# Attention layers of a graph network: other softmax groups, and four pieces of work moved in their engines' orders

## The chip, the cores and the metric

The kernel runs on one core of one Trainium2 chip. A core has five engines that run side by side, each through its own list of instructions, in order: TensorE (PE in the profile, its weight loads PEld), VectorE (DVE), ScalarE (ACT), GpSimd (POOL) and SyncE (SP). They wait for each other on semaphores. The metric is the time of one execution in device microseconds (us). Before the change it is 5247.03 us, the median of 3 runs (5243.42 to 5260.6).

## The reference, cut to what matters

A network of four graph layers over 50000 nodes of 128 features and 25000 edges. The first one is five attention layers (GAT), and only their code is changed. Each of the five computes, with a self loop at every node:

```python
def _gat_layer(x, src, dst, edge_attr_full, W, att, b, ew, eb):
    edge_emb = edge_attr_full @ ew.T + eb
    xw = x @ W
    xj = xw[src].reshape(-1, H, D) + edge_emb.reshape(-1, H, D)
    xi = xw[dst].reshape(-1, H, D)
    alpha = einsum(xi, att_i) + einsum(xj, att_j)     # two heads
    alpha = leaky_relu(alpha, 0.2)
    amax = segment_max(alpha, dst)
    ea = exp(alpha - amax[dst])
    denom = segment_sum(ea, dst)
    alpha = ea / (denom[dst] + EPS)
    aggr = segment_sum(xj * alpha[..., None], dst)
    return aggr.mean(axis=1) + b
for l in range(5):
    h = _gat_layer(h, ...)
    if l < 4: h = relu(h)
```

The edges are sorted by destination. So the softmax over a node's edges is a running maximum and a running sum along the list, and a node's row is needed only where it has edges.

## The kernel before, in words

The 25000 edges lie in 196 tiles of 128, and two tiles make a pair: a layer works through 98 pairs. The layers run one after the other, each in a block of its own (`gat_layer`, called five times), because a layer gathers the rows that the last one has written.

Pair by pair, "step i" of each engine:

- GpSimd gathers the source row of each edge, one indirect DMA for a tile, two for a pair, into a ring of 24 pairs (`RG`). It waits only for a free place in the ring, and each group of pairs has its own semaphore (`g_in`).
- SyncE loads the nodes' own rows (`load_own`), five pairs ahead, stores result rows, and for each group loads masks and edge features (`load_group`), in layers 2 to 5 also the values at run ends (`load_fill_of`), and stores statistics (`store_ends`).
- ScalarE in step i evicts the aggregation of pair i (`evict`), applies ReLU to the mix of pair i-1 (`relu`), evicts edge sums, copies the rows of pair i-2 (`to_rows`), for one step of a group takes exp, and then multiplies gathered rows by their softmax weights (`weigh`), up to two pairs in a step and at most four pairs ahead.
- VectorE makes one-hot matrices of the edges' places (`one_hot`, eight pairs ahead), adds the node's own part (`with_own`), and copies pieces.
- TensorE in step i multiplies weighted rows by one-hots (`aggregate`, L1716), sums edge features in bursts (`sum_edges`), mixes pair i-1 with the weights (`mix`, L1744 and L1745) and turns pair i-2 to rows (`to_rows`, L1757).

The softmax is not made pair by pair but for a group of pairs, one lane for each tile and head, so that up to 56 lanes of VectorE share one instruction. `GAT_PAIRS` lists the groups' sizes. Group g+1 is made ready while group g is worked on, at steps that `GAT_STEPS` sets, counted within group g: at "source" VectorE adds the scores of the gathered rows (`source_scores`, L1358, for which all gathers of group g+1 must have landed) and TensorE turns them (`turn_scores`, L1700); at "scores" VectorE computes the running maximum (`scores`, L1395 to L1401) and ScalarE exp (L1588); at "weights" VectorE computes sums and quotients (`weights`, L1408 to L1417) and TensorE turns them (`turn_weights`, L1706); at "take" VectorE copies them out of PSUM (`take_weights`, L1424). Only then can ScalarE weigh (L1599). Group 0 is prepared before the loop, with nothing beside it. In TensorE's step the turning of the weights stands behind `aggregate` and ahead of `mix`. ScalarE weighs pairs of the next group from the step ahead of "weights". The own scores of a group (`own_scores`) are made in the second step of the group before.

There is no planner: each engine's loop is written out in Python, and the tables above and the places of the calls set the order.

Of the kernel before, what the change touches and what calls it, by code (L numbers as in the profile page):

```python
# [15 lines left out]
P = 128  # L16
# [1140 lines left out]
EdgeBurst = namedtuple("EdgeBurst", "first pairs group")  # L1157
GAT_PAIRS = (4, 12, 14, 14, 14, 14, 14, 12)
GAT_STEPS = ((1, 2, 3, 3), (8, 9, 11, 11), (9, 10, 12, 13), (8, 9, 11, 12), (6, 8, 10, 11), (5, 7, 9, 10), (5, 7, 9, 10), (0, 0, 0, 0))

# [8 lines left out]
def edge_bursts(C):  # L1169

    most = GM // 2
    out = []
    for g, G in enumerate(softmax_groups(C)):
        for k in range(0, G.pairs, most):
            out.append(EdgeBurst(G.first + k, min(most, G.pairs - k), g))
    return out


def gat_layer(nc, K, I, l):
# [3 lines left out]
    NP = C // 2  # L1183
    groups, bursts = softmax_groups(C), edge_bursts(C)
# [9 lines left out]
    with ExitStack() as ctx:  # L1194
# [55 lines left out]
        with nc.Block(no_gpsimd_drain=True) as block:  # L1250
# [86 lines left out]
            def _(eng):  # L1337
                step = Order(eng, s.step)
                eng.memset(aggE[:, :, 2 * P:4 * P], 0.0).then_inc(s.padded, 1)
                eng.memset(prE[:, :, :, :, :], 0.0).then_inc(s.zeroed, 1)  # L1340
                if l > 0:
# [4 lines left out]
                    back = seq4[:, ::-1]  # L1346
                    eng.tensor_tensor_scan(back, K.q.goes[0:4, ::-1], back, 0.0, ALU.mult, ALU.add).then_inc(s.seq, 1)

                def source_scores(g):
# [147 lines left out]
                def runs_weights():  # L1497
# [6 lines left out]
                    eng.tensor_tensor(AS, EL, AS, ALU.mult).then_inc(s.weights, 1)  # L1504

                own_scores(0)
                own_scores(1)
                for i in range(EARLY):
                    one_hot(i)
                source_scores(0)  # L1510
# [72 lines left out]
            def _(eng):  # L1583
# [68 lines left out]
                for i in range(NP + 2):  # L1652
# [16 lines left out]
                    if i < NP:  # L1669
                        if steps_at(g, k, "scores"):  # L1670
                            exp(g + 1)
                        for _ in range(2):
                            if weighed_to < NP and weighed_to <= i + 4 and (at(weighed_to)[0] == g or k >= groups[g].steps["weights"] - 1):
                                weigh(weighed_to)
                                weighed_to += 1
# [11 lines left out]
            def _(eng):  # L1687
# [76 lines left out]
                for i in range(NP + 2):  # L1764
                    if i < NP:
# [7 lines left out]
                        if steps_at(g, k, "source"):  # L1773
                            turn_scores(g + 1)
                        if steps_at(g, k, "weights"):
                            turn_weights(g + 1)
                    if i == NP - 6:
# [19 lines left out]
                    if 2 <= i:  # L1797
                        to_rows(i - 2)

                eng.wait_ge(s.px, NP)  # L1800
# [1631 lines left out]
```

## Time and profile before

| | us |
|---|---|
| median of 3 runs | 5247.03 |
| the profiled execution, its own time | 5250.73 |
| its span | 5249.0 |
| TensorE busy | 4269.4 |
| VectorE busy | 4034.0 |
| ScalarE busy | 3328.7 |
| GpSimd busy | 3228.0 |
| the five attention layers, from 1571 to 3401 us | 1830 |

A layer takes 363 to 369 us. In the third (2302 to 2671) TensorE is busy 303.8 us, VectorE 260.7, ScalarE 255.8, GpSimd 213.1, and the granted TensorE clock is 0.93 of full. The page counts instructions by line of the kernel; "L806" is the helper of all gathers. A row of the timeline gives the start from the beginning of the span, the length, the engine, the line, what is written and read, and in brackets how long the engine had been idle and what ended that.

### The profile page before, as it was taken

Reading aid. Unit: us, or ns where it says so; the run is one execution under the profiler, and the core shown is the slowest. Engines: PE = TensorE matmul, PEld = TensorE weight load, DVE = VectorE, ACT = ScalarE, POOL = GpSimd, SP = SyncE. Lnnn points to the kernel's source line nnn. Section 1 sums busy time; section 2 is a strip of 40 time slices with the busy share of each in tenths; the row PEclk is TensorE's granted clock in tenths of the full one; section 3 lists DMA queues with packets and bytes.
Section 4 is the critical chain, followed back from the end, with each engine's and each line's share of the span. In section 5 each row is a group of like instructions: output and inputs, shape, how many; then the busy total and the mean of one; then the engine's idle time right before and its main releaser. Section 6 shows DMA issues by size and latency. Waiting matters only on the chain. (4 is left out here: it accounts for less than half of the span.)

```text
span 5249.0 us, 101811 instructions
## 1 busy us (share of the span) xinstructions
PE 4269.4 (81%) x28013; PEld 3696.3 (70%) x28013; DVE 4034.0 (77%) x14947; ACT 3328.7 (63%) x9065; POOL 3228.0 (61%) x2905
## 2 busy tenths in 40 slices
PE   4899999999976978969969959877895868879575
PEld 4777777778866867858858848644775857757475
DVE  5799999999986767767757767687566968859765
ACT  2777777777755857847847848644774547768400
POOL 2888888877777727637457367222752247666277
PEclk6999999999988989989989979955997989989755
DMA  3999997666645646636636546488773759857332
GB/s 91 186 221 221 221 220 221 220 221 207 212 155 127 144 86 132 135 77 142 128 89 141 113 102 148 100 246 239 163 144 85 198 158 246 242 125 134 72 94 85
DMA packets 1107279, 825.55 MB, mean 157 GB/s; under 512 B 209510, under 2 KB 1068202, under 8 KB 1106396
## 3 DMA queue, kind: packets, MB, share of 16 engines
q1 hardware_dynamic: 1026800, 690.47, 50.7%
q0 software_dynamic: 77040, 128.08, 12.7%
q8 instruction: 235, 3.85, 0.3%
q14 instruction: 324, 2.65, 0.2%
q10 hardware_dynamic: 2880, 0.50, 0.1%
HBM read 374.78 MB, written 448.11 MB: 157 GB/s over the span
## 5 line engine op out<-in xcount | busy, mean ns | idle before, releaser
L806 POOL DMA_INDIRECT gat_G<-table,k_src_row x980 | 1072.8, 1095 | 316.5 <-issue 282.2
L1599 ACT ACTIVATE gat_Gw<-gat_G,gat_al 128x128 f32<-128x128 f32 x1960 | 618.5, 394 | 88.9 <-DVE gat_al L1424 88.9
L1455 DVE SCALAR_TENSOR_TENSOR gat_Gw<-gat_own,gat_al,gat_Gw 128x128 f32<-128x128 f32 x1960 | 554.7, 343 | 69.2 <-ACT gat_Gw L1599 69.0
L1716 PE MATMUL gat_psG<-gat_ends_at,gat_Gw 128*128 128x128 f32 x3920 | 538.1, 282 | 43.7 <-DVE gat_Gw L1455 43.6
L1744 PE MATMUL gat_psZ<-gat_aggT,t_gat_wh 128*128 128x256 f32 x1960 | 526.3, 392 | 15.3 <-ACT gat_hT L1625 14.9
L1716 PEld LDWEIGHTS gat_psG<-gat_ends_at,gat_Gw 128*128 128x128 f32 x3920 | 493.4, 197 | 54.9 <-DVE gat_Gw L1455 51.9
L635 PEld LDWEIGHTS nodes_psR<-t_ident_v,nodes_hTl 128*128 128x128 f32 x3168 | 431.7, 192 | 105.5 <-issue 1.8
L635 PE MATMUL nodes_psR<-t_ident_v,nodes_hTl 128*128 128x132 f32 x3168 | 446.1, 278 | 0.0
L479 POOL TENSOR_TENSOR nodes_rstd<-nodes_var,k_half 128x14 f32<-128x14 f32 x140 | 365.7, 2612 | 127.0 <-DVE nodes_var L546 127.0
L1625 ACT ACTIVATE gat_hT<-gat_psZ,t_gat_bias 128x256 f32<-128x256 f32 x490 | 231.1, 472 | 267.4 <-PE gat_psZ L1745 261.9
L1744 PEld LDWEIGHTS gat_psZ<-gat_aggT,t_gat_wh 128*128 128x128 f32 x1960 | 340.1, 194 | 56.1 <-ACT gat_aggT L1606 17.2
L1606 ACT ACTIVATE gat_aggT<-gat_psG 128x512 f32<-128x512 f32 x490 | 285.8, 583 | 41.0 <-PE gat_psG L1716 30.8
L1745 PE MATMUL gat_psZ<-gat_aggE,t_gat_ewT 128*128 128x256 f32 x980 | 299.1, 388 | 0.0
L806 POOL DMA_INDIRECT nodes_xg<-in_x,first_dst_tm x196 | 194.8, 994 | 144.6 <-POOLq L84 95.8
L730 ACT ACTIVATE nodes_rows<-nodes_psR 128x396 f32<-128x396 f32 x528 | 263.3, 499 | 30.4 <-PE nodes_psR L635 5.2
L719 ACT ACTIVATE nodes_hTl<-nodes_psY,t_gat_bias 128x384 f32<-128x384 f32 x264 | 153.2, 580 | 178.5 <-PE nodes_psY L645 157.7
L484 POOL DMA_INDIRECT row_of<-first_slot_row_tm,k_node_tm x196 | 222.9, 1137 | 59.7 <-issue 59.4
L1757 PEld LDWEIGHTS gat_psR<-t_ident_v,gat_hT 128*128 128x128 f32 x1568 | 240.5, 193 | 20.5
L523 DVE TENSOR_SCALAR nodes_n<-nodes_xs,nodes_negmean,nodes_rstd 128x128 f32<-128x128 f32 x792 | 245.3, 399 | 4.5 <-issue 2.3
L806 POOL DMA_INDIRECT hgt_edge_G<-table,k_src_row x196 | 186.7, 953 | 100.6 <-ACT hgt_edge_hm L2144 53.5
L806 POOL DMA_INDIRECT cat_edge_G<-table,k_src_row x196 | 194.0, 990 | 84.6 <-ACT cat_edge_hm L2144 41.4
L3189 POOL DMA_INDIRECT out<-cat_sums_rows,k_node_tm x196 | 198.5, 1013 | 77.4 <-issue 57.3
(672 smaller groups left out, 12721.8 us busy)
## 6 DMA issues: line engine op xcount, KB each, us to landing
table<-nodes_rows SPq DMA_DIRECT2D x660, 198.0 KB
table<-nodes_n SPq DMA_DIRECT2D x396, 192.0 KB
gat_own<-table SPq DMA_DIRECT2D x490, 132.0 KB
table<-gat_rows SPq DMA_DIRECT2D x392, 132.0 KB
nodes_x<-in_x SPq DMA_DIRECT2D x132, 192.0 KB
out<-nodes_x_out SPq DMA_DIRECT2D x132, 192.0 KB
gat_G<-table,k_src_row POOLq DMA_INDIRECT x980
hgt_q<-enter_q SPq DMA_DIRECT2D x98, 144.0 KB, 2.2
```

Of the source, the lines that this page charges most:

```text
L479: eng.tensor_tensor(rstd[:, k % 4, :], var[:, k % 4, :], K.half[:, 0:M], ALU.pow).then_inc(s.pow, 1)
L523: ins = eng.tensor_scalar(to[:, t, 0:D], of[:, t, :], negmean[:, k % 4, at + t:at + t + 1], rstd[:, k % 4, at + t:at + t + 1], ALU.add, AL ...
L635: mm = eng.matmul(psR[n % 2][:, t * ROWW:(t + 1) * ROWW], hTl[l][:, t * P:(t + 1) * P], K.ident_v[:, l, :], start=True, stop=True)
L730: eng.activation(rows[:, l - 1, b % 2, :, :], wide(psR[n % 2], T, ROWW), ACT.Copy).then_inc(s.rows_out, 1)
L806: eng.indirect_dma_start(to, None, table, bass.IndirectOffsetOnAxis(ap=index, axis=0)).then_inc(sem, 16)
L1455: ins = eng.scalar_tensor_tensor(Gw[:, i % RS, t, h, :], own[:, i % RO, t, 0:D], al[:, g % 2, 1, a:a + 1], Gw[:, i % RS, t, h, :], ALU.mul ...
L1599: ins = eng.activation(Gw[:, i % RS, t, h, :], G[:, i % RG, t, 0:D], ACT.Copy, scale=al[:, g % 2, 0, a:a + 1])
L1606: eng.activation(aggT[:, i % RA, :, :, :].rearrange("p t h q -> p (t h q)"), psG[i % 2][:, :], ACT.Copy).then_inc(s.aggT, 1)
L1716: mm = eng.matmul(o[:, h * P:(h + 1) * P], Gw[:, i % RS, t, h, :], ends_at[:, i % RE, t, :], start=True, stop=True)
L1744: eng.matmul(o, K.gat_wh[:, l, h, :], aggT[:, i % RA, :, h, :], start=(h == 0), stop=False)
L1745: eng.matmul(o, K.gat_ewT[:, l, k % EDGE_ROWS, :], aggE[:, b % 2, c:c + 2 * P], start=False, stop=True).then_inc(s.mixed, 1)
L1757: mm = eng.matmul(o, of, K.ident_v[:, l + 1, :], start=True, stop=True)
```

## The change

It does five things, all in the attention layers:

- Groups: 4, 6, 9, 11, 12 and four of 14 pairs in place of 4, 12, five of 14 and 12: nine groups for eight, with new steps for them. For groups of 4 and of 14 pairs the step tables are partly those of before.
- Bursts of edge sums are cut into equal parts (`edge_bursts`), so 9 pairs make 4 and 5, not 7 and 2.
- VectorE: the eight early one-hots come ahead of the own scores of groups 0 and 1, and the two memsets behind the sequence scan.
- TensorE: the weights are turned at the end of the step, behind `mix` and `to_rows`.
- ScalarE: pairs of the next group are weighed from the step "take" on, not from the step ahead of "weights".

```diff
-GAT_PAIRS = (4, 12, 14, 14, 14, 14, 14, 12)
-GAT_STEPS = ((1, 2, 3, 3), (8, 9, 11, 11), (9, 10, 12, 13), (8, 9, 11, 12), (6, 8, 10, 11), (5, 7, 9, 10), (5, 7, 9, 10), (0, 0, 0, 0))
+GAT_PAIRS = (4, 6, 9, 11, 12, 14, 14, 14, 14)
+GAT_STEPS = ((1, 2, 3, 3), (3, 4, 5, 5), (5, 6, 7, 8), (7, 8, 9, 10), (7, 8, 10, 11), (8, 9, 11, 12), (6, 8, 10, 11), (5, 7, 9, 10), (0, 0, 0, 0))
...
     for g, G in enumerate(softmax_groups(C)):
-        for k in range(0, G.pairs, most):
-            out.append(EdgeBurst(G.first + k, min(most, G.pairs - k), g))
+        n = (G.pairs + most - 1) // most
+        for k in range(n):
+            a, b = G.pairs * k // n, G.pairs * (k + 1) // n
+            out.append(EdgeBurst(G.first + a, b - a, g))
...
                 step = Order(eng, s.step)
-                eng.memset(aggE[:, :, 2 * P:4 * P], 0.0).then_inc(s.padded, 1)
-                eng.memset(prE[:, :, :, :, :], 0.0).then_inc(s.zeroed, 1)
                 if l > 0:
                     eng.memset(seq4[:, :], 0.0).then_inc(s.seq, 1)
...
                     eng.tensor_tensor_scan(back, K.q.goes[0:4, ::-1], back, 0.0, ALU.mult, ALU.add).then_inc(s.seq, 1)
+                eng.memset(aggE[:, :, 2 * P:4 * P], 0.0).then_inc(s.padded, 1)
+                eng.memset(prE[:, :, :, :, :], 0.0).then_inc(s.zeroed, 1)
...
+                for i in range(EARLY):
+                    one_hot(i)
                 own_scores(0)
                 own_scores(1)
-                for i in range(EARLY):
-                    one_hot(i)
                 source_scores(0)
...
-                            if weighed_to < NP and weighed_to <= i + 4 and (at(weighed_to)[0] == g or k >= groups[g].steps["weights"] - 1):
+                            if weighed_to < NP and weighed_to <= i + 4 and (at(weighed_to)[0] == g or k >= groups[g].steps["take"]):
                                 weigh(weighed_to)
...
                             turn_scores(g + 1)
-                        if steps_at(g, k, "weights"):
-                            turn_weights(g + 1)
...
                     if 2 <= i:
                         to_rows(i - 2)
+                    if i < NP and steps_at(g, k, "weights"):
+                        turn_weights(g + 1)
```

TensorE, first layer, the last step of group 0 and the start of group 1. L1716 (L1718 after) aggregates a pair, L1706 (L1708) turns the weights, L1744, L1745 and L1757 (two lines later after) mix and make rows, L1731 sums edge features, L1695 turns own scores. Before:

```order
L1716 MATMUL gat0_psG1<-gat0_ends_at,gat0_Gw 128x128 x4
L1706 MATMUL gat0_psT<-k_ident,gat0_alB 128x48 x2
L1744 MATMUL gat0_psZ<-gat0_aggT,t_gat_wh 128x256 x2
L1745 MATMUL gat0_psZ<-gat0_aggE,t_gat_ewT 128x256
L1757 MATMUL gat0_psR1<-t_ident_v,gat0_hT 128x132 x2
L1716 MATMUL gat0_psG0<-gat0_ends_at,gat0_Gw 128x128 x4
L1731 MATMUL gat0_psE1<-gat0_ends_at,gat0_wex 32x128 x14
L1695 MATMUL gat0_psT<-k_ident,t_sc_a 56x128 x2
```

After:

```order
L1718 MATMUL gat0_psG1<-gat0_ends_at,gat0_Gw 128x128 x4
L1746 MATMUL gat0_psZ<-gat0_aggT,t_gat_wh 128x256 x2
L1747 MATMUL gat0_psZ<-gat0_aggE,t_gat_ewT 128x256
L1759 MATMUL gat0_psR1<-t_ident_v,gat0_hT 128x132 x2
L1708 MATMUL gat0_psT<-k_ident,gat0_alB 128x24 x2
L1718 MATMUL gat0_psG0<-gat0_ends_at,gat0_Gw 128x128 x4
L1733 MATMUL gat0_psE1<-gat0_ends_at,gat0_wex 32x128 x12
L1697 MATMUL gat0_psT<-k_ident,t_sc_a 36x128 x2
```

The turning of the weights has moved behind the mix and the rows, and holds 24 lanes instead of 48.

VectorE at the start of the second layer. L1376 to L1387 (two lines later after) are own scores, L1441 (L1443) the one-hots, L1358 the scores of gathered rows. Before:

```order
L1376 TENSOR_TENSOR gat1_vb<-gat1_psT,gat1_mk 48x256
L1379 SCALAR_TENSOR_TENSOR gat1_vb<-gat1_mk,gat1_vb 48x128 x2
L1383 SCALAR_TENSOR_TENSOR gat1_vb<-gat1_mk,gat1_fill,gat1_vb 48x128 x4
L1386 SCALAR_TENSOR_TENSOR gat1_lp<-gat1_vb,t_lane_c 48x128
L1387 SCALAR_TENSOR_TENSOR gat1_lp<-gat1_lp 48x128
L1441 TENSOR_TENSOR gat1_ends_at<-k_iota,k_endpos 128x256 x8
L1358 TENSOR_TENSOR gat1_sq<-gat1_G,t_edge_sc 128x16
```

After:

```order
L1348 MEMSET gat1_aggE 128x2x256
L1349 MEMSET gat1_prE 128x256
L1443 TENSOR_TENSOR gat1_ends_at<-k_iota,k_endpos 128x256 x8
L1378 TENSOR_TENSOR gat1_vb<-gat1_psT,gat1_mk 16x256
L1381 SCALAR_TENSOR_TENSOR gat1_vb<-gat1_mk,gat1_vb 16x128 x2
L1385 SCALAR_TENSOR_TENSOR gat1_vb<-gat1_mk,gat1_fill,gat1_vb 16x128 x4
L1388 SCALAR_TENSOR_TENSOR gat1_lp<-gat1_vb,t_lane_c 16x128
L1389 SCALAR_TENSOR_TENSOR gat1_lp<-gat1_lp 16x128
```

The one-hots have moved from behind the own scores of both groups to ahead of them, with the memsets just ahead.

ScalarE, first layer, from exp of group 3 to the weighing of its first pairs (L1599, L1601 after; x4 is one pair, x8 two). L1606 evicts an aggregation, L1625 is ReLU, L1634 the row copy. Before, in group 2 of 14 pairs:

```order
L1588 ACTIVATE gat_ee<-gat_ee 56x256
L1606 ACTIVATE gat_aggT<-gat_psG 128x512
L1625 ACTIVATE gat_hT<-gat_psZ,t_gat_bias 128x256
L1634 ACTIVATE gat_rows<-gat_psR 128x264
L1599 ACTIVATE gat_Gw<-gat_G,gat_al 128x128 x8
L1606 ACTIVATE gat_aggT<-gat_psG 128x512
```

After, in group 2 of 9 pairs:

```order
L1590 ACTIVATE gat_ee<-gat_ee 44x256
L1608 ACTIVATE gat_aggT<-gat_psG 128x512
L1627 ACTIVATE gat_hT<-gat_psZ,t_gat_bias 128x256
L1636 ACTIVATE gat_rows<-gat_psR 128x264
L1608 ACTIVATE gat_aggT<-gat_psG 128x512
L1627 ACTIVATE gat_hT<-gat_psZ,t_gat_bias 128x256
L1636 ACTIVATE gat_rows<-gat_psR 128x264
L1601 ACTIVATE gat_Gw<-gat_G,gat_al 128x128 x8
L1608 ACTIVATE gat_aggT<-gat_psG 128x512
```

One more step of evictions now stands between exp and the weighing.

## Rows read from the trace of the kernel before

**Rows 1.** Waits of the layers, 1571 to 3400: total, times, longest.

```profile
DVE gat_sq L1358 <- DMA gat_G<-table,k_src_row: 153.2, 24, 19.1
...
PE gat_psT L1706 <- DVE gat_alB L1417: 79.6, 40, 6.1
```

**Rows 2.** Timeline, third layer, a regular step: start, length, engine, line.

```profile
2388.78 0.41 DVE L1441 TENSOR_TENSOR gat_ends_at<-k_iota,k_endpos 128x256 f32<-128x256 f32 x1
...
2389.12 1.12 DVE L1455 SCALAR_TENSOR_TENSOR gat_Gw<-gat_own,gat_al,gat_Gw 128x128 f32<-128x128 f32 x4
...
2390.49 1.05 PE L1716 MATMUL gat_psG<-gat_ends_at,gat_Gw 128*128 128x128 f32 x8
...
2391.39 1.03 PE L1744 MATMUL gat_psZ<-gat_aggT,t_gat_wh 128*128 128x256 f32 x4
...
2393.13 1.05 PE L1716 MATMUL gat_psG<-gat_ends_at,gat_Gw 128*128 128x128 f32 x8
...
2393.33 0.39 ACT L1634 ACTIVATE gat_rows<-gat_psR 128x264 f32<-128x264 f32 x1
```

**Rows 3.** Timeline: scores of gathered rows, groups 0 and 1 of layer 1, group 1 of layer 3.

```profile
1583.45 0.18 DVE L1358 TENSOR_TENSOR gat_sq<-gat_G,t_edge_sc 128x16 f32<-128x16 f32 x1 [1.49 <-DMA gat_G<-table,k_src_row]
...
1613.76 0.21 DVE L1358 TENSOR_TENSOR gat_sq<-gat_G,t_edge_sc 128x48 f32<-128x48 f32 x1 [19.11 <-DMA gat_G<-table,k_src_row]
...
2345.80 0.21 DVE L1358 TENSOR_TENSOR gat_sq<-gat_G,t_edge_sc 128x48 f32<-128x48 f32 x1 [15.36 <-DMA gat_G<-table,k_src_row]
```

**Rows 4.** Timeline, third layer, the edges behind groups 1 and 2.

```profile
2390.98 0.40 ACT L1588 ACTIVATE gat_ee<-gat_ee 56x256 f32<-56x256 f32 x1
...
2392.70 0.41 DVE L1408 TENSOR_TENSOR_SCAN gat_f<-gat_mk,gat_ee 56x128 f32<-56x128 f32 x1
...
2395.41 0.32 DVE L1417 TENSOR_TENSOR gat_alB<-gat_alB,gat_mk 56x128 f32<-56x128 f32 x1
...
2396.46 2.45 ACT L1599 ACTIVATE gat_Gw<-gat_G,gat_al 128x128 f32<-128x128 f32 x8 [2.74 <-DVE gat_al L1424]
...
2399.00 1.16 PE L1716 MATMUL gat_psG<-gat_ends_at,gat_Gw 128*128 128x128 f32 x8 [0.94 <-DVE gat_Gw L1455]
...
2406.80 1.16 PE L1716 MATMUL gat_psG<-gat_ends_at,gat_Gw 128*128 128x128 f32 x8 [0.88 <-DVE gat_Gw L1455]
...
2439.05 2.45 ACT L1599 ACTIVATE gat_Gw<-gat_G,gat_al 128x128 f32<-128x128 f32 x8 [3.82 <-DVE gat_al L1424]
...
2442.48 1.72 PE L1744 MATMUL gat_psZ<-gat_aggT,t_gat_wh 128*128 128x256 f32 x4 [1.97 <-ACT gat_hT L1625]
```

**Rows 5.** Timeline, third layer: aggregation of pairs 4, 58 and 97.

```profile
2359.49 1.82 PE L1716 MATMUL gat_psG<-gat_ends_at,gat_Gw 128*128 128x128 f32 x8
...
2532.18 1.05 PE L1716 MATMUL gat_psG<-gat_ends_at,gat_Gw 128*128 128x128 f32 x8
...
2648.17 1.05 PE L1716 MATMUL gat_psG<-gat_ends_at,gat_Gw 128*128 128x128 f32 x8
```

**Rows 6.** Timeline: last gather and last scores of layers 1, 3 and 5.

```profile
1844.87 0.94 POOL L806 DMA_INDIRECT gat_G<-table,k_src_row  x1 [0.30 <-issue]
...
1849.45 0.28 DVE L1358 TENSOR_TENSOR gat_sq<-gat_G,t_edge_sc 128x40 f32<-128x40 f32 x2 [1.01 <-DMA gat_G<-table,k_src_row]
...
2573.95 0.94 POOL L806 DMA_INDIRECT gat_G<-table,k_src_row  x1 [0.30 <-issue]
...
2587.27 0.28 DVE L1358 TENSOR_TENSOR gat_sq<-gat_G,t_edge_sc 128x40 f32<-128x40 f32 x2
...
3314.85 1.01 POOL L806 DMA_INDIRECT gat_G<-table,k_src_row  x1 [0.30 <-issue]
...
3320.93 0.27 DVE L1358 TENSOR_TENSOR gat_sq<-gat_G,t_edge_sc 128x40 f32<-128x40 f32 x2
```

**Rows 7.** Timeline, third layer: one gather and VectorE beside it.

```profile
2568.62 1.08 DVE L1434 TENSOR_TENSOR gat_wex<-gat_ex,gat_al 128x896 f32<-128x896 f32 x1
2568.62 2.23 POOL L806 DMA_INDIRECT gat_G<-table,k_src_row  x1 [0.30 <-issue]
```

## The prediction

> **What bounds the kernel now.** I read the page first and then only the five attention layers, since the change touches nothing else. The profiled execution took 5250.7 us (span 5249.0); the three timed runs had a median of 5247.0, so I work in the profiled execution and take 3.7 off at the end. "k" is the place of a pair in its group, "weights of g" the softmax of group g.
>
> I then looked for what TensorE and VectorE wait for in the layers. VectorE waits 153.2 us for gathered rows, in 24 waits, and TensorE 79.6 us for softmax weights in 40 waits [rows 1]. Next I took the third layer in order of time. TensorE repeats a step of 2.64 us for each pair (starts 2390.49 and 2393.13) with no gap in it: here TensorE is the bound [rows 2]. Two things break the rhythm. One is the start: after two pairs VectorE sits 15.36 us until the 32 gathers of groups 0 and 1 have landed, in the first layer 19.11 us [rows 3]. The other is the edge between groups: there the softmax chain runs through VectorE, ScalarE, VectorE, TensorE, VectorE, ScalarE and VectorE before TensorE has work again [rows 4]. From the first pair of group 1 (pair 4, 2359.49) to pair 58 (2532.18) 172.7 us pass for 54 pairs [rows 5]; 54 x 2.64 is 142.6, so the edges cost 30.1 us there.
>
> There is a second bound beside TensorE: the stream of 196 gathers of each layer. It runs ahead nearly free, and the last group's scores cannot be made before it has landed. In the first layer this is the limit already (last gather issued at 1844.87, VectorE goes on at 1849.45 after 1.01 us of waiting); in the third the scores come at 2587.27, 13.3 us after the last issue at 2573.95, and did not wait [rows 6].
>
> **The change, part by part (third layer).**
>
> *Smaller first groups.* Group 1 needs 20 gathers landed in place of 32. 24 gathers took 1613.76 - 1583.45 = 30.3 us in the first layer, 1.26 each [rows 3], so 12 fewer are 15.2 us: VectorE's scores of group 1 come at 2330.6 instead of 2345.80. Then the old chain took 13.7 us to the first pair of group 1 (2359.49). In the new order TensorE turns the weights after a mix and a row product (from 2391.39 to the next aggregation at 2393.13, 1.7 us, [rows 2]), which then stand between; most of it lies in its wait for the weights, and I charge 0.6. Pair 4 starts at 2330.6 + 14.3 = 2344.9, which is 14.6 us earlier.
>
> *What a group costs TensorE beyond 2.64 us a pair.* Its first two pairs take 2406.80 - 2399.00 = 7.8 us instead of 5.3 [rows 4]: 2.5, with the first burst of edge sums, the turning of own scores and 0.9 of waiting for VectorE's own scores. A second burst (1.1) and the turning of scores (0.3) make 3.9, or 2.8 for the six-pair group with one burst.
> The end of a group is where the table of steps decides. ScalarE's exp stands behind the row copy, 3.2 us after TensorE's start of that pair (2393.33 + 0.39 against 2390.49, [rows 2]), exp 0.4 more, and the weights on VectorE 3.0 (2392.70 to 2395.73; exp and these in [rows 4]). With the weights one step after the scores, as in new groups 1, 2 and 3, VectorE has to wait for exp: the pair after takes place 3.65 + 3.0 + 1.6 (one-hot 0.4, own part 1.1, [rows 2]) = 8.3 us after the scores' pair instead of 5.3, so 3.0. With the take in the last step, as in new groups 1 to 4, ScalarE can weigh the next group's first pair only behind its row copy of the last pair: 3.2, then from there weighing, own part and aggregation as between 2396.46 and 2399.00, 2.6; 5.8 us instead of 2.64, so 3.2. I get for groups 1 to 5: 8.4 (both in one step, and VectorE enters without a lead: 5.6 + 2.8), 10.2, 10.2, 8.6, 5.1: 42.5 us over their 52 pairs.
> So pair 56 starts at 2344.9 + 52 x 2.64 + 42.5 = 2524.7. Before, pair 58 started at 2532.18, so pair 56 at about 2526.9. Of the 14.6 us gained at the start some 2 are left: before, groups 1 to 4 paid 30.1 us, now five groups pay 42.5.
>
> *Weights turned at the end of the step.* The 79.6 us in 40 waits hold five starts; of the rest TensorE fills up to 1.7 us each with a mix and a row product. Where the next pair hangs on the weights (take last) this gives nothing, since those products lay in the bubble before too. After pair 56 it gives about 0.7 at each of two edges. Cover gone: were the weights ready earlier, their turning would come up to 1.7 us late, and VectorE's take with it.
>
> *Weighing from the step of taking.* Before, ScalarE stood 3.82 us at the weighing with its evictions behind it, and TensorE then waited 1.97 for ReLU output [rows 4]. That wait goes. In groups that take in the last step the weighing itself is the path (the 3.2 above), and I have counted that. For the later groups (take in step 10 of 14) nothing changes, because the window of four pairs ahead opens there anyway.
>
> *One-hots first, memsets later.* Eight one-hots (0.4 us each, [rows 2]) and two memsets move into VectorE's wait for masks; group 0 starts about 3 us sooner in layers 2 to 5. But scores of group 1 then wait for gathers until 2330.6 anyway, so I take nothing; it is 0 to 1 us.
>
> *One more group.* One more set of mask, edge and statistic transfers on SyncE's queue, which own rows and result rows share, and one more set of VectorE's softmax work; where the path sees them they are in the group costs, and SyncE loads own rows five pairs ahead. Lanes fall from 48 to 24 in group 1, which scans do not reward.
>
> From pair 58 to pair 97 the old kernel took 2648.17 - 2532.18 = 116.0 us [rows 5]; the new one has 41 pairs from pair 56: 116.0 + 5.3 - 1.4 = 119.9, so pair 97 starts at 2644.6, 3.6 us earlier.
>
> *Clock.* In [rows 4] the mix at 2442.48 has 1.72 us for the four products that take 1.03 in [rows 2]: TensorE was granted 1.2 GHz there instead of 2.4 after its waits at the edge. The new kernel has two more edges with such waits; at 0.7 for the mix and, as an estimate from it, 0.5 for the products behind it I charge one of them, 1.2 us. The Trainium skill, "TensorE: Matmul & The Clock Gate", section "HAM oscillation", says that a kernel which idles between bursts falls to half clock again and again; by it every new edge would pay, 1.2 us more a layer than I charge. The trace agrees for some edges (here) and not for others: [rows 4] has one at full clock at 2399.00.
>
> The layer comes to -3.6 + 1.2 = -2.4 us. I take it for layers 2, 3 and 4: -7.2. Layer 1 ends on its gathers before and after: -0.5. Layer 5 has only a little room before its gathers (scores at 3320.93, last gather issued at 3314.85, [rows 6]): -2. Sum -9.7; 5250.7 - 9.7 = 5241.0, less 3.7 for the median: **5237 us**.
>
> **Rivals.** A gain or loss within 0.3% (15.7 us, about what a measurement of this kernel can tell from none) is no change.
> *Gathers are the bound and the edges cost little.* For it: VectorE and TensorE overlap more than my chains allow, and the first groups' steps stand close to when their gathers land. Then each layer ends on the last gather: landing 4.6 us after issue (1844.87 to 1849.45), the scores can come at 2578.5 instead of 2587.27 in layer 3 (8.7) and at 3319.4 instead of 3320.93 in layer 5 (1.5); half-way between, 5.1, in layers 2 and 4, none in layer 1: 20.3 us, **5227**. With landings 2 us shorter and layers 2 and 4 like layer 3 it would reach 5214.
> *The gather stream gets longer.* Row: a gather beside the weighted edge features (VectorE, 1.08 us) took 2.23 us, against 0.94 for the one at 2573.95 [rows 6, 7]. VectorE's work now begins to press the stream some 15 us sooner, while its amount up to the last gather stays: at most 2 us a layer, which cancels the forecast: **5247**. The skill's page "SBUF — State Buffer", section "Who interferes with whom", would have it otherwise: it says that tensor_tensor does not stall the descriptors of such a DMA; by it this rival is void. The row speaks against the page.
> *Slower.* Place: the edges of new groups 1 to 4. If each of these four falls to 1.2 GHz after its wait (where I charged one more), three more at 1.2 us and VectorE, without a lead, passing on 1 us at each, that is +6.6 a layer against -2.4: +4 in four layers, and in layer 1 its end stays; 5247 + 17 = **5264**. It decides from the point where the edges of groups 1 to 5 cost over 46 us together. Against it: the third layer now has edges at full clock.
> *The change does not do what it says*: the first stall only moves to the scores of group 2 or 3. Against it: the 40 further gathers of groups 2 and 3 end at 2330.6 + 40 x 1.26 = 2381, and TensorE comes to the step of those scores (pair 15) at 2344.9 + 11 x 2.64 + 8.4 + 3.6 = 2386. This is close; its price is under 2 us a layer.
>
> **Numbers.** Forecast (edges eat the start) 0.48; gathers bound 0.28; longer stream or moved stall 0.10; slower 0.14. The forecast's own range is 5228 to 5250. For 8 in 10 the range is 5214 to 5263. Faster by over 0.3%: 0.28 and a slice of the forecast, 0.34; slower 0.14 and a slice, 0.18; the rest 0.48.
>
> **What will show it.** VectorE's wait for gathers before the scores of group 1 should fall from 15 to 19 us to 3 to 6. Pair 4 should again start some 14 us behind those scores, and both some 15 us sooner. Steps of 7 to 10 us should stand at the four edges up to pair 42, with TensorE idle before aggregation and ScalarE's longest waits for weights gone. Pair 56 decides: within 2 us of before, I am right; 6 or more earlier, the gathers bind and VectorE waits before the last group's scores in every layer. A layer that is shorter by over 5 us, or longer by any amount, makes the prediction wrong.

## The result and the profile after

The changed kernel takes 5287.12 us (median of 4 runs, 5283.89 to 5289.31) against 5245.23 of the kernel before in the same session: ratio 1.0079, interval 1.0065 to 1.0094. It is slower by 0.8%, some 42 us. The forecast of 5237 had the wrong sign, and the time lies above its range.

The profiled execution of after took 5283.9 us. From the two traces I took, for each layer, the starts of a few aggregations. Summed over the five layers, us:

| stretch | before | after |
|---|---|---|
| first gather to pair 0 | 127.5 | 116.9 |
| pair 0 to pair 4 | 153.8 | 82.3 |
| pair 4 to 42 | 612.3 | 727.1 |
| pair 42 to 56 | 214.0 | 219.2 |
| pair 56 to 97 | 603.8 | 593.8 |
| pair 97 to the next layer's first gather | 117.2 | 132.1 |
| attention layers | 1828.7 | 1871.4 |

The start gave its 82 us. The 38 pairs after it took 115 us more, the ends of the layers 15 more. (From the last layer's end on, the profiled run of after was some 12 us shorter. Over the traces of all the kernels here, whose code is the same there, that part takes 1832.5 to 1852.4 us, counted from the last attention instruction; no run says why.)

The third layer by stretches, of the kernel before and then of after. The columns are the stretch, its length, busy time of each engine with its instructions, TensorE's granted clock as a share of 2.4 GHz, share of DMA, GB/s. First pairs 4 to 42 and pair 42 to 97 of before:

```profile
2359.50:2484.00 124.50, 113.67 (x861) 103.96 (x861) 93.23 (x375) 97.18 (x282) 97.09 (x90) 0.98 0.68 143
2484.00:2648.20 164.20, 158.82 (x1228) 146.39 (x1227) 128.57 (x497) 139.22 (x403) 70.39 (x63) 1.00 0.58 119
```

The same of after:

```profile
2363.30:2509.00 145.70, 123.99 (x856) 110.04 (x856) 105.00 (x404) 97.54 (x283) 109.12 (x104) 0.93 0.59 130
2509.00:2672.70 163.70, 159.32 (x1234) 146.44 (x1235) 128.43 (x502) 137.68 (x400) 72.64 (x64) 1.00 0.55 119
```

In the first stretch TensorE is busy for 10.3 us more with nearly the same products at a mean clock of 0.93 instead of 0.98, and is idle for 21.7 instead of 10.8 us. The second stretch is as long as before. Time at 1.2 GHz (half clock) between pairs 4 and 97 is 116 us in the five layers after, 33 before.

Waits of after in the layers (us, times, longest), which answer to [rows 1]:

```profile
PE gat_psG L1718 <- DVE gat_Gw L1457: 144.5, 102, 3.0
PE gat_psT L1708 <- DVE gat_alB L1419: 42.8, 22, 6.2
...
DVE gat_sq L1360 <- DMA gat_G<-table,k_src_row: 49.7, 20, 5.4
```

TensorE's waits for weights fell from 79.6 to 42.8 us, but those for the weighted rows, the next thing behind them, rose from 43.6 to 144.5. VectorE's wait for gathers fell from 153.2 to 49.7.

The edge behind group 3 in the timeline of the third layer (start, length, engine, line), which answers to [rows 4]:

```profile
2459.60 0.24 DVE L1426 COPY gat_al<-gat_psT 128x96 f32<-128x96 f32 x1
...
2461.33 0.60 ACT L1608 ACTIVATE gat_aggT<-gat_psG 128x512 f32<-128x512 f32 x1 [3.91 <-PE gat_psG L1718]
2463.71 0.47 ACT L1627 ACTIVATE gat_hT<-gat_psZ,t_gat_bias 128x256 f32<-128x256 f32 x1 [1.79 <-PE gat_psZ L1747]
...
2464.45 2.43 ACT L1601 ACTIVATE gat_Gw<-gat_G,gat_al 128x128 f32<-128x128 f32 x8
...
2465.75 1.14 DVE L1457 SCALAR_TENSOR_TENSOR gat_Gw<-gat_own,gat_al,gat_Gw 128x128 f32<-128x128 f32 x4 [4.58 <-ACT gat_Gw L1601]
...
2466.94 2.08 PE L1718 MATMUL gat_psG<-gat_ends_at,gat_Gw 128*128 128x128 f32 x8 [2.81 <-DVE gat_Gw L1457]
```

ScalarE has the weights from 2459.8 on, but its first weighing of the new group stands behind eviction, ReLU and row copy of the old group's last pair, and between these it is idle for 3.91 and 1.79 us. TensorE then waits 2.81 us in one piece; the forecast had such a wait, as a step that is 3.2 us longer than a regular one. What the forecast charged at one edge only is what follows: the aggregation takes 2.08 us instead of 1.16. (It is four products, and each stands as two records in the trace, so x8.) The edge behind group 2 shows it at its worst:

```profile
2423.15 2.08 PE L1718 MATMUL gat_psG<-gat_ends_at,gat_Gw 128*128 128x128 f32 x8 [2.84 <-DVE gat_Gw L1457]
2425.16 1.92 PE L1733 MATMUL gat_psE<-gat_ends_at,gat_wex 128*32 128x128 f32 x20
...
2427.42 1.92 PE L1746 MATMUL gat_psZ<-gat_aggT,t_gat_wh 128*128 128x256 f32 x4
```

The first step of the group takes 6.9 us (to 2430.07). At 2.4 GHz it takes 4.1, as an experiment below shows. It is not so after every such wait: the kernel has 25 of them, of 2.78 to 2.95 us, ahead of the first aggregation of groups 1 to 5 in five layers, and after 20 of them some or all of the next step runs at 1.2 GHz.

### The profile page after: what moved, and what is told of

It is laid out like the page before. It is cut to its first block and busy times, and to the rows that moved or that the text cites. A ratio compares the mean times of both kernels' runs of the same rounds, so it can differ in the third digit from the quotient of the medians.

```text
span 5282.2 us, 102107 instructions
## 1 busy us (share of the span) xinstructions
PE 4315.1 (82%) x28038; PEld 3719.1 (70%) x28038; DVE 4045.0 (77%) x15096; ACT 3333.7 (63%) x9075; POOL 3254.9 (62%) x2905
## 5 line engine op out<-in xcount | busy, mean ns | idle before, releaser
L806 POOL DMA_INDIRECT gat_G<-table,k_src_row x980 | 1055.2, 1077 | 359.0 <-issue 285.1
L1718 PE MATMUL gat_psG<-gat_ends_at,gat_Gw 128*128 128x128 f32 x3920 | 551.1, 285 | 144.9 <-DVE gat_Gw L1457 144.5
L1601 ACT ACTIVATE gat_Gw<-gat_G,gat_al 128x128 f32<-128x128 f32 x1960 | 612.8, 396 | 22.0 <-DVE gat_al L1426 22.0
L1718 PEld LDWEIGHTS gat_psG<-gat_ends_at,gat_Gw 128*128 128x128 f32 x3920 | 495.0, 198 | 167.0 <-DVE gat_Gw L1457 164.3
L484 POOL DMA_INDIRECT row_of<-first_slot_row_tm,k_node_tm x196 | 238.7, 1218 | 59.7 <-issue 59.1
L806 POOL DMA_INDIRECT k_src_row<-row_of,first_src_tm x196 | 223.7, 1141 | 58.2 <-issue 55.4
L806 POOL DMA_INDIRECT cat_edge_G<-table,k_src_row x196 | 194.4, 992 | 83.2 <-issue 39.9
```

The source lines that it names most:

```text
L484: eng.indirect_dma_start(K.row_of, bass.IndirectOffsetOnAxis(ap=K.node_tm[:, c:c + 1], axis=0), K.slot_row_tm[:, c:c + 1], None, bounds_ch ...
L806: eng.indirect_dma_start(to, None, table, bass.IndirectOffsetOnAxis(ap=index, axis=0)).then_inc(sem, 16)
L1601: ins = eng.activation(Gw[:, i % RS, t, h, :], G[:, i % RG, t, 0:D], ACT.Copy, scale=al[:, g % 2, 0, a:a + 1])
L1718: mm = eng.matmul(o[:, h * P:(h + 1) * P], Gw[:, i % RS, t, h, :], ends_at[:, i % RE, t, :], start=True, stop=True)
```

## The experiments

**1. The new groups alone.**

```diff
 before.py
-GAT_PAIRS = (4, 12, 14, 14, 14, 14, 14, 12)
+GAT_PAIRS = (4, 6, 9, 11, 12, 14, 14, 14, 14)    # with their GAT_STEPS and even bursts
```

> The kernel before with the nine new groups, their steps and the even edge bursts, and without the three moves. Theory (the edges of the small groups cost more than the earlier start gives): the whole loss is here, 5285 to 5300 us, ratio 1.008 to 1.011; pair 4 of layer 3 starts some 14 us earlier, pairs 4 to 42 take over 110 us more in the five layers, and the tail of a layer is longer by about 3 us. Rival (the three moves cost it, by turning weights late and weighing late): the groups alone are within 0.3% of before, 5235 to 5255.

Measured 5265.17 us, ratio 1.0026 (1.0013 to 1.0038). Pairs 4 to 42 took 79.4 us more in the five layers and the ends 14.4. So the groups carry a third of the loss only. Neither text had it right: the loss is shared. Time at half clock between pairs 4 and 97 is 90.5 us here, against 33 before and 116 in the changed kernel, so most of the rise comes with the groups, without any move.

**2. The three moves alone.**

```diff
 before.py, TensorE
-                        if steps_at(g, k, "weights"):
-                            turn_weights(g + 1)
...
                     if 2 <= i:
                         to_rows(i - 2)
+                    if i < NP and steps_at(g, k, "weights"):
+                        turn_weights(g + 1)
 ScalarE
-k >= groups[g].steps["weights"] - 1
+k >= groups[g].steps["take"]
```

The third move, VectorE's one-hots first and memsets later, is made as in the change and not repeated here.

> The kernel before with the three moves of order alone (weights turned at the end of TensorE's step, weighing from the step of taking, one-hots ahead of own scores and memsets later), groups and bursts as before. Theory (small groups): within 0.3% of before, 5235 to 5250, since ScalarE's long weighing waits go but nothing else. Rival (moves cost): 5265 to 5285.

5266.07 us, ratio 1.0033 (1.0018 to 1.0047). My theory fell here too: the moves cost by themselves. Pairs 4 to 42 took 26.4 us more, pairs 42 to 97 17.2 less. One-hots first brings pair 0 forward by 10 us in the five layers, and pair 4 waits for the gathers and takes all of it back, as forecast: 282.7 us from the first gather to pair 4, against 281.3 before.

**3. TensorE kept busy at the edges.**

```diff
 after.py
+                def keep_warm(i, n):
+                    for _ in range(n):
+                        eng.matmul(psG[(i + 1) % 2][:, 0:2 * P], K.gat_wh[:, l, 0, :], aggT[:, (i - 1) % RA, :, 0, :], start=True, stop=True)
...
+                    if edge and k == groups[g].pairs - 1:
+                        keep_warm(i, 4)
                     if i < NP and steps_at(g, k, "weights"):
                         turn_weights(g + 1)
+                    if edge and k == groups[g].pairs - 1:
+                        keep_warm(i, 9)
```

> The changed kernel with idle-time products added on TensorE at the ends of groups 0 to 4: 4 of 256 columns at the end of the last step but one, 4 ahead of the turning of the weights and 9 behind it, into a PSUM bank that the next aggregation overwrites. Nothing else changes. Theory that the fall to 1.2 GHz at the edges is half of the loss: time at half clock between pairs 4 and 97 falls from 116 us to under 60 in the five layers, and the kernel from 5287 to 5255 to 5270. Rival (the wait itself is the cost and the clock only goes with it): half-clock time falls, but the time stays within 5 us of 5287, or rises by the products that run past the wait.

5317.14 us, ratio 1.0123 (1.0093 to 1.0153): slower than the changed kernel. Edges are the ends of groups 0 to 4; each gets 4 products at the end of the last step but one, which the diff above leaves out, and 13 in the last. Half-clock time between pairs 4 and 97 was 0, yet pairs 4 to 42 of layer 3 took 148.1 us. The 13 products behind the last row products ran for 5.78 us, past the weighed rows. I had counted 0.21 us for one; it is 0.44. So this run could not tell the two readings apart.

**4. The same with products that fit the wait.** 2, 2 and 4 in place of 4, 4 and 9.

> The changed kernel with fewer idle-time products at the ends of groups 0 to 4: 2 after the last step but one, 2 ahead of the turning of the weights and 4 behind it. In the run before this one such a product of 256 columns took 0.43 us, not 0.21, and 9 of them ran past the wait of 2.8 us; 4 take 1.7 us and fit. Theory that the clock is part of the loss: half-clock time between pairs 4 and 97 stays near 0 (116 us in the changed kernel), pairs 4 to 42 take some 137 us a layer (145.7), and the kernel 5250 to 5265 us. Rival (the chain of the weighing is the cost, the clock only goes with it): pairs 4 to 42 stay at 143 us or more and the kernel over 5275.

5252.18 us, ratio 0.9998 (0.9988 to 1.0008). The whole loss is gone. The stretch from pair 4 to 42 of the third layer of this kernel:

```profile
2352.30:2490.00 137.70, 128.80 (x920) 113.92 (x920) 103.76 (x404) 97.47 (x283) 106.90 (x102) 1.00 0.62 137
```

137.7 us at full clock instead of 145.7 at 0.93. Its edge behind group 2 (the products are L1764):

```profile
2407.23 2.75 PE L1764 MATMUL gat_psG<-gat_aggT,t_gat_wh 128*128 128x256 f32 x12
2410.21 1.16 PE L1718 MATMUL gat_psG<-gat_ends_at,gat_Gw 128*128 128x128 f32 x8 [0.23 <-DVE gat_Gw L1457]
2411.30 1.06 PE L1733 MATMUL gat_psE<-gat_ends_at,gat_wex 128*32 128x128 f32 x20
...
2412.53 1.03 PE L1746 MATMUL gat_psZ<-gat_aggT,t_gat_wh 128*128 128x256 f32 x4
```

The aggregation starts no earlier than it would have: 2.8 us pass between the end of the last row products (2406.78 + 0.61) and it, as in the changed kernel. Only the clock differs, and the step takes 4.1 us instead of 6.9. Half-clock time between pairs 4 and 97 is 3.4 us instead of 116, and pairs 4 to 42 take 39.0 us less in the five layers. So the lower clock behind these waits is the cause of the loss, shown. With it held the kernel is level with before, not 10 us faster as forecast; before itself spends 33 us at half clock and got no such products.

**5. Late turning alone, and weighing from the take alone.** The first or the second edit of 2, on the kernel before, without the one-hots first.

> The kernel before with one move alone: the weights are turned at the end of TensorE's step, behind the mix and the row products. Theory (this move only shifts products into a wait): within 5 us of before. Rival (it makes VectorE's take 1 to 2 us late at every edge whose weights are ready): 5255 to 5270, with the loss spread over all seven edges.

5262.95 us, ratio 1.0014 (1.0004 to 1.0024): 10 us over before's median of 5253.3 beside it, a small loss. The time is in the rival's range, but the loss is not spread over all edges, as the rival had it: pairs 4 to 42 took 9.9 us more in the five layers, pairs 56 to 97 took 7.2 less, the ends 5.5 more. The edge behind group 1 in the third layer of before, ahead of the aggregation at 2399.00 in [rows 4]:

```profile
2395.79 0.33 PE L1706 MATMUL gat_psT<-k_ident,gat_alB 56*128 56x56 f32 x2 [1.60 <-DVE gat_alB L1417]
```

With late turning alone:

```profile
2424.10 1.16 PE L1716 MATMUL gat_psG<-gat_ends_at,gat_Gw 128*128 128x128 f32 x8 [2.88 <-DVE gat_Gw L1455]
2425.19 1.89 PE L1731 MATMUL gat_psE<-gat_ends_at,gat_wex 128*32 128x128 f32 x28
```

The waits of 1.60 and 0.94 us have become one of 2.88, and the step takes 5.7 us instead of 4.1. Between pairs 4 and 42 TensorE is idle for 48.7 us in the five layers against 49.9 before, and yet at half clock for 59.4 us against 27.9.

> The kernel before with one move alone: ScalarE weighs the next group's first pairs from the step of the take, not from one step before the weights. Theory (where the take is in the last step, the first aggregation of the next group then waits 2.8 us in one piece behind eviction, ReLU, row copy and weighing, and TensorE starts it at 1.2 GHz): this move carries the loss of the three, 5260 to 5270 us. Rival (it only takes away ScalarE's wait of 3.8 us): 5235 to 5247.

5302.03 us, ratio 1.0097 (1.0080 to 1.0113): this move alone costs more than all three together, and more than the theory had. The trace, of the fastest of its four runs, has 45.4 us at half clock between pairs 4 and 42 but 71.6 us of idle time, so here it is the waiting more than the clock; experiment 6 shows the path.

**6. The changed kernel without late turning, and without the late weighing.**

> The changed kernel with the turning of the weights put back to the middle of TensorE's step; groups, weighing and one-hots stay changed. If the late turning costs at the small groups' edges (where TensorE waits 1.2 us for it behind products that it could have done in the wait after it), 5287 falls to 5265 to 5275; if the weighing from the take is what costs, it stays within 6 us of 5287.

5354.08 us, ratio 1.0203 (1.0179 to 1.0227), against 1.0079 with late turning. Neither case came: late turning saves the change from worse. The edge behind group 1 in this kernel's third layer:

```profile
2415.08 0.42 PE L1708 MATMUL gat_psT<-k_ident,gat_alB 36*128 36x36 f32 x2 [3.01 <-DVE gat_alB L1419]
2415.44 2.07 PE L1746 MATMUL gat_psZ<-gat_aggT,t_gat_wh 128*128 128x256 f32 x4
...
2418.40 0.47 ACT L1627 ACTIVATE gat_hT<-gat_psZ,t_gat_bias 128x256 f32<-128x256 f32 x1 [5.69 <-PE gat_psZ L1747]
...
2419.57 2.43 ACT L1601 ACTIVATE gat_Gw<-gat_G,gat_al 128x128 f32<-128x128 f32 x8
```

TensorE stands 3.01 us at the turning with the mix behind it, makes the mix at half clock (2.07), and only then can ScalarE do ReLU, row copy and weighing: 11.0 us from one group's last aggregation (2411.02) to the next group's first (2422.06), against 6.4 in the changed kernel (2381.88 to 2388.32). With late turning the mix is done inside the wait.

> The changed kernel with weighing put back to one step before the weights; groups, late turning and one-hots stay. Together with three kernels that have run it tells what the two moves do on the new groups: none of the two 1.0026, weighing alone 1.0203, both 1.0079. Theory (weighing from the take is the costly one and late turning softens it): this one 1.000 to 1.004, 5250 to 5272. Rival (late turning costs by itself on small groups): 1.006 or more, over 5283.

5277.05 us, ratio 1.0052 (1.0031 to 1.0072), between the two texts. The four together, on the new groups: neither move 1.0026, late turning 1.0052, late weighing 1.0203, both 1.0079. On the old groups: turning 1.0014, weighing 1.0097, all three 1.0033. The two kernels with both moves and the two of this experiment have the one-hots first as well, the others do not; experiment 2 saw them give nothing by pair 4.

**7. Another table of steps.**

```diff
 after.py, GAT_STEPS of groups 2 to 7
-(5, 6, 7, 8), (7, 8, 9, 10), (7, 8, 10, 11), (8, 9, 11, 12), (6, 8, 10, 11), (5, 7, 9, 10)
+(5, 6, 7, 8), (4, 6, 8, 9), (4, 6, 8, 9), (5, 7, 9, 10), (5, 7, 9, 10), (5, 7, 9, 10)
```

The steps of group 6 become earlier too, by one, which the expectation does not name.

> The changed kernel with another table of steps: groups 3 to 5 (11, 12 and 14 pairs) take at step 9 of 11, 9 of 12 and 10 of 14 instead of the last or last but two, and their own scores, scores and weights come earlier (4, 6, 8). Theory (a take in the last step costs 2.8 us of waiting and often the clock): two edges a layer lose that wait, 5287 falls by 15 to 30 us, to 5257 to 5272. Rival (the bound is VectorE's and ScalarE's softmax work itself, wherever it stands): within 5 us of 5287. Second rival (the earlier scores wait for gathers): slower than 5287, with VectorE's wait for gathers up from 49.7 us to over 80.

5252.03 us, ratio 1.0010 (0.9996 to 1.0024): 35 us of the 42 are back, more than expected. The edges behind groups 3 and 4 have no wait of 2.8 us; in exchange TensorE waits 68.6 us for scores (33.7 in the changed kernel). The second rival's sign came without its loss: VectorE waits 144.1 us for gathers.

> The changed kernel with the earlier table of steps for groups 3 to 5 and 5 idle-time products behind the turning of the weights in the last step of groups 0, 1 and 2. Theory (edge waits and clock are two separate parts of the loss): 5225 to 5240, 12 to 25 us below the same steps without the products (5252). Rival (the steps already take away the edges at which the clock fell): 5245 to 5255.

5247.22 us, ratio 1.0005 (0.9992 to 1.0018), not told apart from the version without products (1.0010): the rival's time, but not its reason. Half-clock time between pairs 4 and 42 fell from 71.7 us to 47.8, yet that stretch took 692.9 us against 693.5, and VectorE's waits for gathers rose from 144.1 to 184.1: with these steps the scores wait for the gathers, and what the clock gives is spent there. Behind the waits for scores, 5.91 us at pair 34, the clock still falls.

**8. The old groups and the moves, kept busy.** Experiment 2 with 5 products behind the turned weights in the last step of groups 0, 1 and 2.

> The kernel before (its eight groups) with the three moves and 5 idle-time products of 256 columns behind the turning of the weights in the last step of groups 0, 1 and 2. Theory (the moves lose only through the clock at these edges; after pair 42 they gain 17 us in five layers): half-clock time between pairs 4 and 97 falls from 64 us to under 20, and the kernel to 5228 to 5242, faster than before by 0.2 to 0.5%. Rival (the moves cost through the wait of 2.8 us itself): 5255 to 5266 as without the products.

5235.88 us, ratio 0.9980 (0.9968 to 0.9991), against 1.0033 without the products; half-clock time between pairs 4 and 97 is 0. The third layer from pair 4 to 42, of the moves alone and then with the products:

```profile
2368.90:2497.10 128.20, 117.00 (x860) 105.73 (x860) 94.01 (x373) 96.77 (x281) 98.03 (x92) 0.96 0.63 139
```

```profile
2361.60:2484.50 122.90, 116.28 (x880) 105.49 (x880) 93.58 (x373) 96.86 (x281) 96.07 (x89) 1.00 0.66 143
```

So moves and products together are faster than both kernels. How much of the 0.2% the moves give is open, since no run put the products into the kernel before, which spends 33 us at half clock itself. For the moves speaks that pairs 42 to 97, where no products stand, take 802.6 us against 817.8 before; against them, that pairs 4 to 42 take 610.1 without any time at half clock, and 612.3 before with 27.9 us of it.

**9. An earlier start without a further edge.** Groups of 4, 10, 14, 14, 14, 14, 14, 14, the three moves, even bursts, the last burst's copies late; with the 5 products and without.

> The three moves with eight groups of 4, 10, 14, 14, 14, 14, 14 and 14 pairs (no edge more than before; even bursts; the last burst's copies behind the run sums), and 5 idle-time products behind the turning of the weights in the last step of groups 0, 1 and 2. Group 1 needs 4 gathers less, 5 us at 1.26 us each. Theory (an earlier start without a further edge is kept, and the clock is held): pair 4 starts some 5 us earlier than with 4 and 12, and the kernel takes 5210 to 5230, ratio 0.993 to 0.998. Rival (what is won at the start is lost to the gather stream, to waits for scores of group 2 or in the tail): 5234 to 5245.

5231.51 us, ratio 0.9981 (0.9970 to 0.9991). Pair 4 comes some 25 us earlier in the five layers than in experiment 8, and all is paid back: 18.4 more up to pair 42, 8.6 more in the ends. Mostly the rival's case: no gain over 0.9980 that can be told.

> The same without the idle-time products. Theory (the clock costs some 25 us with the moves, whatever the groups): half-clock time between pairs 4 and 97 over 45 us in the five layers against under 10 with them, and 20 to 30 us slower than with them, 5235 to 5255. Rival (the products gain only with the groups of 4 and 12): within 8 us of the kernel with them.

5250.91 us, ratio 1.0021 (1.0009 to 1.0034), with 58.2 us at half clock between pairs 4 and 97 against 10.2 with the products: the clock costs 0.4% here too (0.5% in 8, 0.8% in 4).

**10. The ends of the layers.**

```diff
 after.py, VectorE
-                        if first_pair == 0:
+                        if first_pair == 0 and b < NB - 1:
                             edge_pieces(b)
+                        if i == NP:
+                            edge_pieces(NB - 1)
```

> The changed kernel with one edit on VectorE: the copies from the last edge burst (four, 0.68 us) are made behind the weights of the run sums, where the kernel before has them, and not ahead of them. Theory that the new place of the last burst (pair 91 instead of 94) makes the tail longer: VectorE's first copy behind the run sums comes 1.9 to 2.4 us after the last aggregation's start instead of 3.1, and the five tails sum to 127 to 129 us instead of 132. Rival (the tail is longer for another reason): under 1 us of change in the five tails. The whole time cannot tell it (3 us).

This kernel ran once, in 5283.25 us. VectorE's first copy behind the run sums came 3.10 us after the last aggregation's start (2677.24 and 2674.14), as in the changed kernel (2675.78 and 2672.69); before it was 1.9. The ends sum to 130.1 us, 2 less, which one trace cannot tell from none. The order of the copies is not what makes that first copy late; why the ends are longer stays open. Every kernel with a last group of 14 has it (128 to 133 us against 117 to 124 with 12).

## Why the prediction was wrong

By its steps, in the third layer, in us:

| step | forecast | measured |
|---|---|---|
| scores of group 1 earlier | 15.2 | 14.5 |
| pair 4, from the first gather | 42.0 | 39.9 |
| groups 1 to 5 over 2.64 a pair | 42.5 | 51.6 |
| the same with the clock held | | 43.7 |
| clock at the edges | 1.2 | 7.9 |
| pair 56 to 97 | 119.9 | 120.5 |
| end of the layer against before | 0 | +2.4 |
| layer against before | -2.4 | +6.5 |

- *Start: right, and better than forecast.* Counted from the first gather (2302.93 before, 2323.36 after), the scores of group 1 came 14.5 us earlier. Pair 4 followed them after 11.6 us where the working had 14.3, so it came 16.6 us earlier and not 14.6. VectorE's scores of group 1 and the aggregation of pair 4 in the layer's timeline, the answer to [rows 3] and [rows 5]:

```profile
2351.74 0.18 DVE L1360 TENSOR_TENSOR gat_sq<-gat_G,t_edge_sc 128x24 f32<-128x24 f32 x1 [3.42 <-DMA gat_G<-table,k_src_row]
...
2363.30 0.94 PE L1718 MATMUL gat_psG<-gat_ends_at,gat_Gw 128*128 128x128 f32 x6 [2.79 <-DVE gat_Gw L1457]
```

- *Chains of the edges: right, with some luck.* With the clock held the five groups cost 43.7 against 42.5: 8.8, 9.5, 10.2, 8.9 and 6.3 us, where the working had 8.4, 10.2, 10.2, 8.6 and 5.1. The stretch from pair 4 to 42 takes 137.8, and the forecast's terms give 38 x 2.64 + 37.4 = 137.7; that they meet so well is errors that cancel. The 5.6 in group 1 and the 8.6 and 5.1 have no sum in the working: its own parts give 3.2 + 3.9 = 7.1 for group 4. The waits of 2.8 us that it had are there.
- *The clock: here it failed.* "The new kernel has two more edges with such waits ... I charge one of them, 1.2 us." The new kernel has, at the edges behind groups 1 to 4, one unbroken wait of 2.8 us each, and after such a wait TensorE mostly works at 1.2 GHz for some or all of the first step: 6.9 us instead of 4.1 at its worst, 5.6 behind group 3. It did not after the fourth of them: that aggregation, at 2509.02, took 1.16 us. Group by group the clock took 0.4, 1.5, 4.5, 1.5 and 0 us. That is 7.9 in this layer, not 1.2; 6.7 of the 8.9 us by which the layer was off. Over five layers the held clock gives 39 us between pairs 4 and 42.
- *The waits were counted but their form was not.* Before, much the same idle time came in pieces, 1.6 before the turning and 0.9 before the aggregation, with products between them, and the clock stayed at 2.4 GHz behind group 1 in every layer. Late turning joins the pieces, and with idle time unchanged the half-clock time between pairs 4 and 42 doubles (experiment 5). That is why the moves cost on the old groups too, where I had them at nothing or a gain. On the new groups the form is not all of it: the groups alone have 80.0 us at half clock in that stretch and 95.4 us idle, the changed kernel 106.3 and 114.4, before 27.9 and 49.9. The Trainium skill, "TensorE: Matmul & The Clock Gate", section "HAM oscillation", which the working set aside for the mild row of before, has the direction right: by it every new edge would pay, 1.2 more than charged. The trace agrees for 20 of the 25 edges of this kind, and the price is higher, 7.9 in the third layer.
- *ScalarE's wait of 3.82 goes: true, and worth little.* Its waits for weights fell from 88.9 us in 25 to 22.0 in 15, and TensorE's for weighted rows rose by 100.9. What is weighed later is also ready later.
- *Late turning gives 0.7 at each of two edges after pair 56: true.* Alone on the kernel before it takes 7.2 us off the pairs 56 to 97 of five layers, 0.7 an edge. What the working had at nothing is the edges that take last: there it costs 9.9 us alone, through the clock, and the whole is a loss of 0.14%. With late weighing it keeps the mix off the path there (1.0079 against 1.0203).
- *The ends of the layers: taken as unchanged*, but 3.0 us a layer longer, and not explained.
- *Rivals.* "Slower" named the right place and condition: over 46 us for groups 1 to 5, it was 51.6. Its price was too small, since it gave each edge 1.2 us of clock where 2 were lost in the mean, and had nothing for the ends. "Gathers are the bound" did not come to pass: the last gather was issued 279.0 us after the first, against 271.0 before. "Gather stream longer" was thus right in direction; with the clock held the last gather is issued at 270.9 again, so the longer stream follows from the slow edges and is not their cause. The row it stood on is no exception: in the trace of before the 37 gathers that overlap the weighted edge features by over 0.25 us took 1.52 us in the median, against 0.94 for those that do not. The stall did not move to the scores of groups 2 and 3: VectorE waits 1.3 and 4.3 us there in the third layer.

## What to carry to other kernels

Where TensorE is the bound, price a wait by its form as well as its length: one unbroken wait of 2.8 us cost up to as much again in the step behind it, and the same idle time in two pieces often did not (1.6 and 0.9 us at the edge behind group 1 of before cost nothing more). An edit that tidies an order by moving products out of the gaps can lose by this; check the granted clock behind each longer gap, and if nothing useful can fill it, products whose result is overwritten do, so long as they end before the wait does. Two moves that are each a loss can be a smaller loss together, so test them in combination. And give the kernel before the same idle-time products, which was not done here: only then is it known what a change is worth once the clock is held. Where the path waits for gathers, as with the earlier steps of experiment 7, a held clock gave nothing.

## What the runs showed of the hardware

- After a wait of 2.8 us the four products of an aggregation took up to 2.08 us and the two of the mix 1.92, at 1.2 GHz, against 1.16 and 1.03 with TensorE busy in the wait, at 2.4 GHz. In the changed kernel time at 1.2 GHz followed 20 of 25 such waits. Single waits of 0.5 to 1.1 us in the rhythm mostly left them at 1.16 and 1.03. Two close together (1.18 and 1.06 at the last pair of group 3) did not, 1.74 and 1.91; two others (1.60 and 0.94 behind group 1 of before) did.
- Eight idle-time products at an edge, two of them in the last step but one and six in the last (2.75 us of work), held the clock at 2.4 GHz from pair 4 to 97 in four of five layers. Four and 13 held it in all, but the 13 took 5.78 us and made the kernel slower. On the old groups five in the last step of groups 0, 1 and 2 held it in all.
- An f32 product stands as two records in the trace, a transposing one (the turning of weights) as one. So 26 records in 5.78 us are 13 products of 256 columns, 0.44 us for one, not 0.22.
